# Moving the context's products of a decoder layer's prologue from behind tile 7 of x to behind tile 11

## The reference

```python
# L0_attn: no softmax, so (q k^T) v can be computed as q (k^T v): it needs sums over all rows of x
attn = jnp.einsum('bhik,bhjk->bhij', q, k)
out = jnp.einsum('bhik,bhkj->bhij', attn, v)
# L0_xattn: Key = Values = ctx_1024, 2 x 154 rows of 512
k = _split_heads(Key @ W_k.T + b_k)
v = _split_heads(Values @ W_v.T + b_v)
scores = jnp.einsum('bhqd,bhkd->bhqk', q, k) / jnp.sqrt(jnp.float32(D_K))
```

## Time and profile before

| | us |
|---|---|
| median of the runs | 927.38 |
| runs | 927.26, 929.71, 927.38 |
| profiled execution, its own time | 927.58 |
| its span | 925.8 |
| PE busy in the span | 908.7 (98%) |
| DVE busy | 707.6 (76%) |
| ACT busy | 545.4 (59%) |
| POOL busy | 500.9 (54%) |
| prologue's end (first PE matmul of the second block) | 116.1 |

### The profile page before, as it was taken

How to read it: one execution, slowest core, us unless ns; L and a number is a source line. 1 busy time by engine, 2 the same in 40 slices (tenths; PEclk the granted TensorE clock), 3 DMA queues, 4 the chain that set the end, 5 groups by cost and what they waited for, 6 DMA issues and landing times.

```text
span 925.8 us, 18979 instructions
## 1 busy us (share of the span) xinstructions
PE 908.7 (98%) x6694; PEld 730.2 (79%) x6694; DVE 707.6 (76%) x1985; ACT 545.4 (59%) x1658; POOL 500.9 (54%) x505
## 2 busy tenths in 40 slices
PE   8999998999999999999999999999999999999997
PEld 7867566667787878888888787878787878787876
DVE  6697456457797979787887878787878787879775
ACT  6555206657665757575856666656575757575631
POOL 1034015657675666657575756666566665756420
PEclk9999999999999999999999999999999999999999
DMA  8791000103000000002101010101010010100001
GB/s 293 244 336 48 23 26 29 38 8 108 15 24 31 25 31 24 31 24 81 29 25 30 25 30 25 30 25 30 24 29 25 12 43 8 47 1 24 1 23 46
DMA packets 30890, 45.65 MB, mean 49 GB/s; under 512 B 2764, under 2 KB 15564, under 8 KB 30540
## 3 DMA queue, kind: packets, MB, share of 16 engines
q1 hardware_dynamic: 26139, 35.26, 11.9%
q10 hardware_dynamic: 4656, 9.18, 2.9%
HBM read 34.10 MB, written 9.70 MB: 47 GB/s over the span
## 4 chain that ended last, share of the span: by engine, by line
PE 73%; DVE 6%; issue 4%; POOL 3%; ACT 2%; POOLq 0%; DVEq 0%; ACTq 0%
PE dense L88 18%; PE dense L90 17%; PE dense L89 17%; PE turned L1501 5%; PE scores L1489 4%; PE rest_value L1515 3%; PE rest_value L1519 3%; PE turned L1398 1%; PE dense L1398 1%; PE rest_value L1507 1%; PE scores L1404 1%; DVE prob L1041 1%; POOL row_inv L1304 1%; ACT prob L756 1%; PE dense L1443 1%
## 5 line engine op out<-in xcount | busy, mean ns | idle before, releaser
L1304 POOL TENSOR_TENSOR row_inv<-row_sum,minus_one 128x4 f32<-128x4 f32 x128 | 145.6, 1138 | 262.5 <-ACT prob L756 260.9
L756 ACT ACTIVATE prob<-prob,row_min 128x154 f32<-128x154 f32 x512 | 209.4, 417 | 20.4 <-DVE row_min L1041 20.4
L1310 POOL TENSOR_TENSOR prob<-prob,row_inv 128x512 f32<-128x512 f32 x128 | 136.4, 1065 | 0.0
L1041 DVE CUSTOM_DVE_ANT_0 prob<-scores,mask_add 128x154 f32<-128x154 f32 x512 | 127.0, 309 | 6.3 <-PE scores L1489 6.2
L764 ACT ACTIVATE prob_t<-turned 128x512 f32<-128x512 f32 x128 | 75.8, 592 | 53.1 <-PE turned L1501 53.1
L756 ACT ACTIVATION_READ_ACCUMULATOR prob<-prob,row_min 128x1 f32 x512 | 98.8, 193 | 0.0
L1501 PE MATMUL turned<-ident,prob 128*128 128x128 f32 x512 | 77.0, 273 | 3.7 <-POOL prob L1310 1.4
L88 PE MATMUL dense<-xt_hi,cross_wq_hi 128*128 128x256 f32 x256 | 75.2, 294 | 1.3 <-DVE xt_lo L1032 1.3
L88 PE MATMUL dense<-mix_k_hi,ffn_wk_hi 128*128 128x256 f32 x256 | 74.6, 291 | 0.0
L1501 PEld LDWEIGHTS turned<-ident,prob 128*128 128x128 f32 x512 | 61.0, 141 | 15.8 <-issue 4.7
L1099 DVE TENSOR_TENSOR k_act_lo<-square,k_act_hi 128x512 fp32r<-128x512 f32 x32 | 51.4, 1606 | 28.8 <-ACT k_act_hi L789 28.8
(11 more groups left out here) (273 smaller groups left out, 2658.9 us busy)
## 6 DMA issues: line engine op xcount, KB each, us to landing
x_rows<-x_rows SPq DMA_DIRECT2D x32, 256.0 KB, 4.4
xt_raw<-x_cols SPq DMA_DIRECT2D x16, 512.0 KB, 3.7
out<-gate_then_y SPq DMA_DIRECT2D x15, 512.0 KB, 2.8
mask_in<-mask SPq DMA_DIRECT2D x16, 154.0 KB, 2.3
cross_wv<-cross_wv SPq DMA_DIRECT2D x2, 512.0 KB, 6.8
cross_wk<-cross_wk SPq DMA_DIRECT2D x1, 1024.0 KB, 9.3
self_wv<-self_wv ACTq DMA_DIRECT2D x1, 1024.0 KB, 8.0
self_wk<-self_wk ACTq DMA_DIRECT2D x1, 1024.0 KB, 11.8
```

What stands on the lines that cost most here:

```text
L756: m = act.activation(keys, keys, ACT.Exp, bias=row_min[:, buf, t, h:h + 1], scale=-1.0, accum_out=row_sum[:, buf, t, h:h + 1])
L1041: m = dve.tensor_tensor_reduce(prob[buf][:, t, h * CTX:(h + 1) * CTX], s_bank[:, h, t * CTX:(t + 1) * CTX], mask_add[n % 2][:, t, :], -SCA ...
L1304: pool.tensor_tensor(row_inv[:, buf, t, :], row_sum[:, buf, t, :], minus_one[:], ALU.pow).then_inc(*p_inv.up)
L1310: pool.tensor_tensor(keys[:, :, 0:P], keys[:, :, 0:P], inv.broadcast_to([P, HPG, P]), ALU.mult).then_inc(*p_norm.up)
```

## The change

In the prologue:

- PE makes the context's values and keys behind tile 11 and not behind tile 7.
- SP's sequence of loads is another: tiles 0 to 4, context, tile 5, first half of `cross_wv`, tiles 6 to 9, second half of `cross_wv`, tiles 10 and 11, `cross_wk`, the two biases, tiles 12 on.
- The splits on ACT and DVE are spread in between: tiles 0 to 5, part 0, tiles 6 and 7, part 1, tiles 8 to 11, parts 2 and 3. ACT then issues the four weight loads, splits tiles 12 to 15, and takes out the keys. DVE does not add tiles 8 to 11 to `x_sum` ahead of their low parts but all four between parts 2 and 3, and it splits tiles 12 and 13 ahead of the values' biases.
- The context is handed over in DRAM as [128 partitions, 4 x 308], so that a partition's data is one run of 4928 bytes and not four of 1232.

```diff
@@ prologue
-    vector_adds = range(HALF + RING)
+    vector_adds, late_adds = range(HALF + RING), range(8, 12)
@@ sp_program
-            for j in range(RING):
+            for j in range(RING + 1):
                 load(j)
-            sp.dma_start(ctx_t[:], wide("ctx_cols")).then_inc(*ctx_in.up)
-            for j in range(RING, 2 * RING):
+            sp.dma_start(ctx_t[:], io["ctx_cols"]).then_inc(*ctx_in.up)
+            load(5)
+            sp.dma_start(w_v[:, 0:KT // 2, :], wide("cross_wv")[:, 0:KT // 2, :]).then_inc(*wv_in.up)
+            for j in range(6, 10):
                 load(j)
-            sp.dma_start(w_v[:, 0:KT // 2, :], wide("cross_wv")[:, 0:KT // 2, :]).then_inc(*wv_in.up)
             sp.dma_start(w_v[:, KT // 2:KT, :], wide("cross_wv")[:, KT // 2:KT, :]).then_inc(*wv_rest_in.up)
+            load(10)
+            load(11)
             sp.dma_start(w_k[:], wide("cross_wk")).then_inc(*wk_in.up)
...
-            for j in range(2 * RING, 5 * RING):
+            for j in range(12, 5 * RING):
                 load(j)
@@ act_program
-            high(0, 1, 2, 3, 4)
+            high(0, 1, 2, 3, 4, 5)
             part_high(0)
-            high(5, 6, 7)
-            for i in range(1, len(to_split)):
-                part_high(i)
+            high(6, 7)
+            part_high(1)
+            high(8, 9, 10, 11)
+            part_high(2)
+            part_high(3)
...
-            high(8, 9, 10, 11)
+            high(12, 13, 14, 15)
...
-            high(12, 13)
             load_row("self_bk")
-            high(14, 15, 16, 17)
+            high(16, 17)
@@ dve_program
+            def add(*tiles):
+                for j in tiles:
+                    b, i = j // HALF, j % RING
+                    dve.wait_ge(*x_here[i].at(j // RING))
+                    if j:
+                        dve.wait_ge(*summed.at(j - 1))
+                    else:
+                        dve.wait_ge(*made.at(1))
+                    dve.tensor_tensor(x_sum[:, b, :], x_sum[:, b, :], x_in[i][:], ALU.add).then_inc(*summed.up)
...
+                    if j in vector_adds and j not in late_adds:
+                        add(j)
...
-            low(0, 1, 2, 3, 4)
+            low(0, 1, 2, 3, 4, 5)
             part_low(0)
-            low(5, 6, 7)
-            for i in range(1, len(to_split)):
-                part_low(i)
-            low(8, 9)
+            low(6, 7)
+            part_low(1)
+            low(8, 9, 10, 11)
+            part_low(2)
+            add(*late_adds)
+            part_low(3)
+            low(12, 13)
...
-            low(*range(10, 18))
+            low(*range(14, 18))
@@ pe_program
-            sums(*range(2 * RING))
+            sums(*range(3 * RING))
...
-            sums(*range(2 * RING, HALF + 2))
+            sums(*range(3 * RING, HALF + 2))
@@ kernel
-        "ctx_cols": flat(a["ctx_1024"].reshape(B * CTX, D).T),
+        "ctx_cols": flat(a["ctx_1024"].reshape(B * CTX, KT, P).transpose(2, 1, 0)),
```

## The result

The changed kernel took 929.48 us (median of 20 runs, 927.47 to 930.86), the kernel before 927.51 (20 runs, 926.67 to 929.71). The ratio is 1.0015, 95% interval 1.0008 to 1.0022: slower by about 1.4 us by the ratio and by 2.0 by the medians. The forecast was 926.5, the range 925.3 to 929.3; the time moved the other way and ended just outside the range. The executions of the changed kernel fall into two groups, 7 of 20 at 927.5 to 927.9 and 13 at 929.0 to 930.9; the profiled one is of the upper group.

A forecast was written before the change was run, and what follows sets the result against it. PE, busy 98% of the span, bounds the kernel, so only its prologue gap could yield: 0.91 us gained at tile 6, 0 to 0.3 lost at tile 8, giving 926.5 us against the median; range 925.3 to 929.3.

The forecast's parts named there:

- The gap and what lies behind it: Prologue: PE's one sizeable wait, before tile 5, makes it 1.79 us late; the second block follows rigidly.
- 3.96 us from the context's high part to PE's tile: Prologue: from ACT's start on the context's high part to PE's start on the waiting tile, 3.96 us, kept for tile 6.
- The same bytes, so I keep 9.87: Tile 5's load: same bytes ahead in SP's queue, so landing stays at 9.87; tile 6 at 14.88, gain 0.91 us.
- The bound taken from tile 4's 4.5 us of landing: Low bound of the gain: tile 5 taking 4.5 us lands at 10.47, leaving 0.31 us gained.
- The new wait in DVE's order: Second key block: biases queue behind tile 13's split; fits with 0.5 to 2.4 us left; as slower rival 930.2, chance 0.12.
- The rule of turns between the queues: DMA engines alternate queues by packet, so tile 13 shares with ACT's weights without waiting for all 3 MB; no wait opens.
- Tile 8's margin: Prologue, tile 8: ready at 17.89, PE wants it at 18.02, 0.13 us left; 0 to 0.3 us lost.
- `cross_wk` was in time: Context's keys: `cross_wk` issued about 16.5, there at 28.3 even at 11.8 us, split at 32.6 when the keys start.
- The weights, read past 50 us: ACT's queue: weight loads issued some 3 to 7 us later, first read past 50 us, costed at nothing.
- The 0.2 us taken off: Final sum: profiled execution 927.58 lies 0.2 over the runs' median 927.38, so 926.7 becomes 926.5.
- The layout: Context's load: longer runs, taken as nothing; estimated 0.1 us from fewer packets, at most a few tenths for tile 5.
- The rival "the wait only changes its place": `cross_wv` behind tile 5 takes its bandwidth, landing 10.5 to 10.8, and tile 8 misses its margin; 927.4, chance 0.19.

The follow-up runs named there:

- `ctx_early`: Changed kernel with the context loaded ahead of tile 4 again, as in the kernel before; 926.69 us, ratio to the kernel before 0.9996.
- both repairs: Changed kernel with the context loaded ahead of tile 4 and DVE adding the values' biases ahead of splitting tiles 12 and 13; 927.09 us, ratio 0.9996.
- `parts_behind_7`: On top of both repairs, context parts split behind tiles 7, 9 and 11, first half of `cross_wv` loaded behind tile 7; 925.98 us, ratio 0.9985.
- `bias_first`: Changed kernel with DVE adding the values' biases ahead of the splits of tiles 12 and 13; 928.16 us, 928.04 in a second session.
- `weights_late`: Changed kernel with the four weight loads on ACT's queue issued behind the splits of tiles 12 to 15; 927.96 us.
- `again`: The changed kernel as it is, run and profiled once more as a base; 929.22 us.

## Why the prediction was wrong

*The gap and what lies behind it: right.* PE's wait for DVE's low part was the one place in the prologue where time could be had, and the second block follows rigidly: 809.6 to 809.8 us of span behind its start in all 14 profiles.

*3.96 us from the context's high part to PE's tile: right.* 12.03 to 15.98 is 3.95, and it is 3.94 or 3.95 in all nine profiles in which PE waited before tile 6.

*"The same bytes, so I keep 9.87": wrong, 1.10 us.* This is the step that cost the gain. The bytes ahead of tile 5 were the same, but not the time at which they were handed to the queue. Tile 5 was issued at 6.09 (5.97 before) and took 4.9 us, not 3.9. The context had been filling the time in which SP stands at tile 4 (72 against 330 GB/s in the stretch shown); with the context ahead of tile 4 again, tile 5 took 4.7, 3.6 and 4.0 us in the profiles of `ctx_early`, of both repairs and of `parts_behind_7`. The bound taken from tile 4's 4.5 us of landing was too low too; tile 5 took 4.9 to 5.3 in the six profiles with the late context and the new layout. The prediction wrote that DMA was busy at 1.05 in the stretch of the gap; that was some seven microseconds past the place in question. The stretch to look at was 4.7 to 6.5 us, with the question what is queued there while SP waits.

*The new wait in DVE's order: seen, priced too low.* The mechanism, its place and the queue behind it were as written, and it made most of the loss: without it (`bias_first`, twice, and `weights_late`) the medians are 0.3 to 0.7 over the kernel before, each with a ratio not told from no change. Two terms were mis-sized. Tile 8's add ended at 25.8 and not at 22.7 to 24.6, so load 13 was issued at 26.70 and not at 23.3 to 25.2: 1.10 us came down from tile 6 through tile 7's split to load 11 (17.16, forecast 16.07), and tile 11 took 4.7 us, just over the upper bound. And tile 13's landing was taken from a load that shared the engines with the weights (6.7) and took 8.4. From tile 13's landing to the end of the bias it took 1.97 us, where 1.9 was forecast. From the bad end of the forecast it adds up: 0.5 in hand, 1.2 more since PE came later itself, less 1.5 for the issue and 1.7 for the landing, is 1.5 short, and 1.63 was measured. The chance given to this case, 0.12, followed from margins that had all been reckoned from the 9.87: the two steps were not independent, and a miss in the first ate into the margin of the second. In the execution of `again` tile 6 was even later and this wait did not open, so it took load 12's place behind the weights as well.

*The rule of turns between the queues.* The Trainium skill ("DMA: Bandwidth & Descriptors", section "Queues, rings and completion order") has the engines take turns between SP's and ACT's queue, from which the prediction read that this wait would not open. The measured landings are 7.7 and 8.4 us behind the weights, 3.1 just ahead of them and 2.6 without them. If turns meant equal shares, 256 KB at half of the 330 GB/s that the engines moved from 26.0 to 33.6 us would take 1.6 us and not 0.8, and the load would land in some 3.4 (an estimate from the 2.6). The measurement decides: equal shares is not what a load gets here, and one handed over 1.1 to 1.4 us behind the first of the weights, with 2 MB of them issued, has to be counted with 4 to 5 us more. How the engines share their time between the queues in those microseconds no run shows.

*Other steps.* Tile 8's margin held (no wait there in any profile). `cross_wk` was in time in all (it landed as late as 25.85, with both repairs). The weights, read past 50 us, could be later at no cost; that they could be in the way of the tiles was missed. The 0.2 us taken off because the profiled execution lies above the median were 0.1 against the median of 20 runs (927.51). The layout was right at "nothing" for the median of the kernel before, and is open within 0.5 us elsewhere.

*The rival "the wait only changes its place"* was right about tile 6, with the wrong mechanism: not `cross_wv` behind tile 5, as its run showed, but the hole ahead of it.

## What to carry to other kernels

When a transfer is moved behind one that has to wait for a buffer, ask what the DMA engines have in their queues during that wait: the bytes may be the same and the landing still later, here by 1.0 to 1.4 us. When work is put ahead of a result that the busiest engine wants, it is the landing of that work's data that sets the price, and its load's place against big transfers on another queue made the difference between 3 and 8 us here, from one execution to the next. And when several margins of a schedule are reckoned from one landing, they fall together; the chances of the rivals should be worked out with that landing late.

## What the runs showed of the hardware

How long tile 12's load of 256 KB on SP's queue took hung on when it was issued against the first of three weight loads of 1 MB on ACT's queue:

| load 12 against the first weight load | us to landing | profiles |
|---|---|---|
| the weights issued later (`weights_late`) | 2.6 | 1 |
| 0.7 us ahead | 2.7 | 1 |
| 0.05 us ahead | 3.1 | 1 |
| 0.2 us behind | 4.2, 4.7 | 2 |
| 0.4 us behind | 5.6 | 1 |
| 1.1 us behind | 6.9 | 1 |
| 1.4 us behind | 7.6 to 7.9 | 4 |

With both repairs load 12 was 2.4 us ahead and took 3.7 us; `cross_wk`, ahead of it in the same queue, was still on its way there. And PE's first matmuls of tile 0 took 0.48 to 0.50 and 0.40 us in six of the 14 profiles and 0.77 to 0.80 and 0.63 in the other eight, of kernels whose PE program up to there is the same, with a granted clock of 1.00 in the table by stretches either way; it moved tile 1 by up to 1.0 us. What sets that was not tried.
